# A two-block transformer kernel: square sums of queries and keys taken six tiles behind the projection, not four

## What is computed

```python
def _causal_conv_silu(x, w):
    Kw = w.shape[1]
    xp = jnp.pad(x, ((0, 0), (Kw - 1, 0), (0, 0)))
    y = sum((w[:, j] * xp[:, j:j + x.shape[1], :] for j in range(Kw)))
    return jax.nn.silu(y)

def _l2_norm(x, eps=EPS):
    n = jnp.sqrt(jnp.sum(x * x, axis=-1, keepdims=True))
    return x / jnp.maximum(n, eps)

q = _causal_conv_silu(x @ Wq.T, conv_q).reshape(Bx, Tx, H, DK)
k = _causal_conv_silu(x @ Wk.T, conv_k).reshape(Bx, Tx, H, DK)
v = _causal_conv_silu(x @ Wv.T, conv_v).reshape(Bx, Tx, H, DV)
q = _l2_norm(q)
k = _l2_norm(k)
```

## Time and profile before

| what | value |
|---|---|
| median of three runs | 9197.6 us |
| the profiled execution | 9196.53 us, its span 9194.7 us |
| mean granted clock of TensorE | 0.886 of full speed |
| TensorE matmul busy | 7044.5 us, 77% |
| VectorE busy | 4897.7 us, 53% |
| ScalarE busy | 2651.0 us, 29% |
| GpSimd busy | 2810.2 us, 31% |
| DMA, 16 engines | q1 7.9% of their span |

### The profile page before, as it was taken

The page is one execution under the profiler, slowest core; times in us unless marked ns, Lnnn a source line. Parts: engine busy times, 40 slices in busy tenths (PEclk is TensorE's granted clock), DMA queues, the critical chain, the costliest instruction groups (busy, mean ns, idle before and its releaser), DMA issues. The chain is left out here.

```text
span 9194.7 us, 157207 instructions
## 1 busy us (share of the span) xinstructions
PE 7044.5 (77%) x57416; PEld 5014.2 (55%) x57416; DVE 4897.7 (53%) x9955; ACT 2651.0 (29%) x5274; POOL 2810.2 (31%) x3681
## 2 busy tenths in 40 slices
PE   6777778777787777877777787777877778777786
PEld 3655646555464554645546465564655546455464
DVE  5546465464654646546464555546546465464653
ACT  2323232232422314223232322313223142231421
POOL 2414233151421414224142331414215142141421
PEclk9888989898898988989889888888989889898897
DMA  1100101001000100001000010010101000000000
GB/s 50 29 22 18 34 15 29 24 20 40 18 19 24 26 33 18 19 30 30 24 18 21 28 29 24 18 41 9 28 24 26 33 18 19 28 22 33 18 19 5
DMA packets 376003, 225.76 MB, mean 25 GB/s; under 512 B 336880, under 2 KB 353392, under 8 KB 366960
## 3 DMA queue, kind: packets, MB, share of 16 engines
q1 hardware_dynamic: 375152, 214.71, 7.9%
HBM read 155.95 MB, written 58.72 MB: 23 GB/s over the span
## 5 line engine op out<-in xcount | busy, mean ns | idle before, releaser
L750 DVE SCALAR_TENSOR_TENSOR SC<-SC,CW 128x512 f32<-128x512 f32 x1536 | 1281.0, 835 | 236.6 <-DVEq L748 144.9
L1406 PE MATMUL PS<-CST,SC 128*128 128x128 f32 x2776 | 502.6, 323 | 634.2 <-PEq L1662 275.2
L938 POOL TENSOR_TENSOR RSTD<-VAR,NHALF 128x2 f32<-128x2 f32 x200 | 150.7, 754 | 2275.4 <-POOLq L937 2267.3
L1406 PEld LDWEIGHTS PS<-CST,SC 128*128 128x128 f32 x2776 | 372.8, 164 | 816.7 <-issue 798.3
L1078 POOL TENSOR_TENSOR FR<-MS,NHALF 128x8 f32<-128x8 f32 x128 | 211.2, 1650 | 1887.9 <-POOLq L1077 1883.5
L1403 PE MATMUL PS<-S,KQ 64*64 64x128 f32 x8192 | 723.7, 294 | 0.0
L1049 POOL TENSOR_TENSOR WO<-WO 128x30 f32<-128x30 f32 (+14 forms) x960 | 614.8, 640 | 136.4
L1046 POOL TENSOR_TENSOR WO<-WO 128x30 f32<-128x30 f32 (+14 forms) x960 | 586.6, 611 | 134.4 <-issue 6.9
L1403 PE MATMUL PS<-XT,WV 128*128 128x512 f32 x1024 | 530.5, 659 | 108.3 <-PEq L1681 70.4
L1403 PE MATMUL PS<-XT,WQK 128*128 128x512 f32 x1024 | 563.1, 685 | 0.0
L1403 PEld LDWEIGHTS PS<-S,KQ 64*64 64x64 f32 x8192 | 516.8, 146 | 82.2 <-issue 78.1
(11 more groups left out here) (157 smaller groups left out, 13232.7 us busy)
## 6 DMA issues: line engine op xcount, KB each, us to landing
WV<-in_wv SPq DMA_DIRECT2D x16, 2048.0 KB, 11.7
WO<-in_wo SPq DMA_DIRECT2D x16, 2048.0 KB, 8.7
WQK<-in_wq SPq DMA_DIRECT2D x16, 1024.0 KB, 5.2
WQK<-in_wk SPq DMA_DIRECT2D x16, 1024.0 KB, 7.4
cells_in<-SC SPq DMA_DIRECT2D x128, 128.0 KB, 2.7
WO<-cells_in SPq DMA_DIRECT2D x32, 512.0 KB, 3.3
cells_out<-WO SPq DMA_DIRECT2D x32, 512.0 KB, 2.6
cells_nat<-WO SPq DMA_DIRECT2D x32, 512.0 KB, 3.9
```

What stands on the lines that cost most here:

```text
L750: op = v.scalar_tensor_tensor(y, pre[:, j:j + G], CW[:, i * TAPS + j:i * TAPS + j + 1], y, ALU.mult, ALU.add)
L938: q.tensor_tensor(out=RSTD[:, 2 * k:2 * k + 2], in0=VAR[:, 2 * k:2 * k + 2], in1=NHALF[:, 0:2], op=ALU.pow).then_inc(rstd_ready, 1)
L1406: return nc.tensor.matmul(out_, in_, ident, is_transpose=True, start=True, stop=True)
```

## The change

`SQ_LAG` is 6. In the stage of q and k, TensorE now does the square sums of tile `i - 6` ahead of projecting tile `i`; the wait for `proj_free` stays four tiles behind. After the last projection it waits once for four `proj_free` and then does the square sums of the last six tiles. ScalarE's square of tile `i` for `i >= 4` now also waits for `sq_free`, which TensorE gives with the last square-sum matmul of tile `i - 4`. In the stage of v the lag stays 4, and there too the four `proj_free` are waited for at once ahead of the last four `after_conv`.

```diff
+SQ_LAG = 6
...
+        sq_free = sem("sq_free")
...
             def square(i):
                 act.wait_ge(qk_ready, 1)
                 act.sem_inc(qk_ready, -1)
+                if i >= 4:
+                    act.wait_ge(sq_free, 1)
+                    act.sem_inc(sq_free, -1)
                 a.activation(SQ[:, (i % 4) * G:(i % 4) * G + G], KQ[:, (i ^ 1) * G:(i ^ 1) * G + G],
                              ACT.Square).then_inc(sq_ready, 1)
...
                         j = mm(bank(4)[:, col:col + 2], SQ[:, (i % 4) * G + t * P:(i % 4) * G + t * P + P], cst("ind"))
+                    if i < QK_TILES - 4:
+                        j.then_inc(sq_free, 1)
                     if i == QK_TILES - 1:
                         j.then_inc(ssq_ps, 1)
...
             def projections(tiles):
+                lag = SQ_LAG if tiles[0] == 0 else 4
                 for i in tiles:
+                    if i >= tiles[0] + lag:
+                        after_conv(i - lag)
                     if i >= tiles[0] + 4:
-                        after_conv(i - 4)
                         pe.wait_ge(proj_free, 1)
                         pe.sem_inc(proj_free, -1)
...
                     j.then_inc(proj_ps, 1)
-                for i in tiles[-4:]:
-                    pe.wait_ge(proj_free, 1)
-                    pe.sem_inc(proj_free, -1)
+                pe.wait_ge(proj_free, 4)
+                pe.sem_inc(proj_free, -4)
+                for i in tiles[-lag:]:
                     after_conv(i)
```

## The result

The changed kernel takes 9208.84 us (median of 20 runs, 9204.36 to 9214.58), against 9197.28 us for 20 runs of the kernel before, taken with them. The ratio is 1.0013, 95% interval 1.0007 to 1.0019. The profiled execution took 9214.58 us, its span 9212.7 us, at a mean granted clock of 0.884 (before: 0.886).

The account below looks back on a forecast made before the run. VectorE paces mid-stage of q and k, TensorE its start and end; line 768 moves the pass. 9196.53 + 65.0 - 30.9 = 9230.6, median said as 9232 us (0.37% slower); range 9210 to 9256.

Parts of the forecast that it names:

- The wait at the start: Start of q and k stage: tile 4 is projected without a gap, its taps start 1.85 us earlier; 30.9 us saved.
- The pile at the end: End of q and k stage: six tiles' square sums in one block at clock 0.50, 4.06 us a pass, 65.0 in all.
- The rivals on the clock: End block's clock comes back within it, 9195 us, chance 0.10; or is full throughout, 9160 us, chance 0.03.
- the wait that stays: Start of q and k stage: the wait remains, so all of the 65.0 us stays; 9263 us, chance 0.04.
- ScalarE's wait at nothing: ScalarE's added wait for `sq_free` in the q and k stage: taken as 0, bounded above by 8.1 us.
- Edits at nothing: ScalarE's wait for `sq_free`, TensorE's signal for it and the v stage's single wait: each taken as 0.
- the one wait for four `proj_free`: End of v stage: met 0.67 us before the transposes of tiles 28 and 29 start, so taken as 0.
- The rest of a pass shifts its clock: From `prepare` on, starting 2.1 us later meets clock changes elsewhere: a microsecond a pass either way; widens range, no own chance.

Follow-up runs that it names:

- e1: Changed kernel, but in both stages each of the last four tiles waits for its own `proj_free` again, so no pile; 9176.31 us, 0.9978 of before.
- e2: Kernel before with its old start, plus one wait for four `proj_free` and a block of six tiles' square sums at the end; 9225.98 us, 1.0034 of before.
- f1: Changed kernel with its one wait for four `proj_free` written as four waits in a row, 6 TensorE instructions more a pass; 9251.37 us, 1.0058 of before.
- g2: Changed kernel with six spare-semaphore instructions added at the end of TensorE's loop body, behind the recurrence; 9214.21 us, 1.0022 of before.
- e3: Kernel before with three needless VectorE multiplications a pass ahead of the scalar part, behind the wait for `ssq_ps`; 9244.74 us, 1.0051 of before.
- e4: Kernel before with five needless VectorE multiplications a pass ahead of the scalar part, behind the wait for `ssq_ps`; 9234.30 us, 1.0042 of before.
- g1: Changed kernel with six spare-semaphore instructions added at the start of TensorE's loop body; 9250.49 us, 1.0053 of before.
- f3: Changed kernel with the wait for four `proj_free` moved ahead of the last tile alone in both stages, so no pile; 9149.70 us, 0.9947 of before.
- f2: Kernel before with both stages' four end waits for `proj_free` merged into one ahead of the last tile, 6 TensorE instructions fewer a pass; 9155.71 us, 0.9956.

## Why the prediction was wrong, point by point

- **The wait at the start, -1.85 us a pass: right.** e1's stage is 1.94 shorter. ScalarE's 2.51 us of waiting for tile 4 is gone, tiles 4 and 5 are projected without a gap, and VectorE's halo wait in that stage fell by the predicted 31 us.
- **The pile at the end, +4.06 a pass: right.** e2's stage is 3.90 longer. The block took 10.37 us (10.62 predicted) after 10.28 of idle time (some 10 predicted), at 0.50 throughout. With both, the stage is 2.04 longer, 30.6 us in 15 passes. The Trainium skill's advice (TensorE: Matmul & The Clock Gate, "Why this matters for your kernels") to keep TensorE busy so that it rises to full clock did not work out in this block: 10.37 us of matmuls of two columns, one after the other, stayed at 0.50, and so did the block of every pass, in e2 as well.
- **The rivals on the clock and on the wait that stays: rightly held unlikely.** None of them shows in the rows.
- **ScalarE's wait at nothing: nothing in the rows speaks against it.** e1 has it and its stage still got the full gain; no run isolates it.
- **"Edits at nothing", the one wait for four `proj_free`: this is the step that failed.** The prediction asked only when the wait would be met: in the stage of q and k it is the pile, priced at 4.06 us, and in that of v it took the edit as 0. It put nothing for the instructions that merging removes. Four waits are four instructions and one is one, and the code behind them lies three instructions earlier, twice. That is worth 42.5 us (f1 against the changed kernel), more than the net 34.1 us that the prediction summed up.
- **"The rest of a pass shifts its clock ... 16 us in all": right in kind for the v stage, and too small.** The v stage got longer by 8.8 us in 15 passes, and it is the passes with a lower clock in its first 8 us that did. What shortened the recurrence was something else. It is mostly of two lengths, about 235 to 236.5 and 237.5 to 240 us, and in most passes one packet decides which (13 of f1's 14 passes with a long spill took over 237 us, and none of g2's 16 did). The two passes 556.9 us apart that the prediction gave for this rival are no case of it: their recurrence took 237.4 us, against 237.8 in the mean of the 15. The stretch from the recurrence to the next stage of q and k is 103 to 105 us behind odd passes and 108 behind even ones, and this pass is odd. Besides, f1 is at 9251, about 20 us above the 9232 that the predicted steps give, and has no fetch gain. Of these, 10 us lie in the recurrence (3576.8 against 3566.4) and 8 in the v stage (969.1 against 960.8). The v stage's part goes with the clock of its first 8 us, as in the rows above; in the recurrence TensorE's wait for the scatter is longer by the same 10 us (68.9 against 58.9), for a reason that no run isolates. e3 and e4, with 1.9 and 3.1 us of delay and 9245 and 9234 us, show that the effect of a later start isn't proportional to it.

So the account of the 11.6 us is: some 33 from the two steps (2.04 us in 16 passes; 34.1 predicted), some 21 from the rest of the pass (in part open), and 42.5 given back by the six instructions a pass, with which the packet left the spill. That the time came as near to the forecast as 23 us is luck: the two parts that the prediction left out have opposite signs.

Left open, too: why the first two passes of the kernel before have the packet late with the same code, why one of the changed kernel's two long spills is long with the packet at 87.9 us, and how the 6 instructions make 1.5 us. TensorE is some 20 matmuls further from the recurrence's start when the packet comes in the changed kernel than before; this was not resolved to the instruction. Some 31 instruction packets fall in a pass and all may move with the six instructions. Only the one at the second spill was followed, so a part of the 42.5 us could belong to others.

## What to carry to other kernels

When a time moves and the stages that the diff touches don't explain it, cut the pass into stretches and look for the one that moved though nothing in it changed; here it held more than the change itself. An edit that adds or drops instructions in a long loop body shifts where the 16 KB instruction packets fall, so count the instructions of each engine before and after, and where a waited-for transfer lies near such a packet, try the edit with the count kept: a few idle instructions ahead of the place tell (g1, g2). Here the change is best kept for its start only, if at all, with the end's waits merged behind the third of the last four tiles: f3, 9149.7 us, 0.9947 [0.9933, 0.9961] of before. The merged waits without the new start, f2, give 9155.7, not clearly more.

## What the runs showed of the hardware that was not expected

- A packet of the instruction queue, 16,384 bytes and about 1 us on one DMA engine, falls together with a 1 MB spill over all 16 engines that takes 5.7 to 6.1 us from issue to scatter instead of 4.7 to 4.8: seven of its packets are left to run alone, one after another, behind the instruction packet.
- The page has 499 such packets before and 498 after, 0.4% of the DMA engines' time; the edits that move one of them off the spill in most passes, and perhaps others with it, are worth 27 to 43 us of 9200.
- A block of 48 passes of 128x2 matmuls, busy for 10.37 us without a gap, ran at a granted clock of 0.50 to its end.
